# Main attention of a two-layer kernel: rows of maxima of two heads in one tile, a third score bank, and the maxima's banks shared

## What is computed

```python
q = (rmsnorm(h @ q_a_w.T) @ q_b_w.T)          # 16 heads: 128 plain + 64 rotary
kv_a = h @ kv_a_w.T                            # 64 latent + 16 x 64 rotary keys
q_pe, k_pe = apply_rope(q_pe), apply_rope(k_pe)
probs = softmax(qf @ kf.T * 192 ** -0.5)       # 1024 x 1024 for each head
main_out = (probs @ v) @ o_w.T
```

## Time and profile before

| | |
|---|---|
| median of 3 runs | 1565.17 us (1564.35 to 1569.16) |
| the profiled execution | 1566.81 us, its span 1565.0 us |
| PE busy | 1426.5 us (91%) in 7287 instructions |
| PEld / DVE / ACT / POOL busy | 54% / 59% / 48% / 35% |
| chain that ended last | PE 36%, DVE 6%, issue 3%, ACT 2% of the span |
| main attention | from about 310 to 930 us |

### The profile page before, as it was taken

The page is one execution under the profiler, slowest core; times in us unless marked ns, Lnnn a source line. Parts: engine busy times, 40 slices in busy tenths (PEclk is TensorE's granted clock), DMA queues, the critical chain, the costliest instruction groups (busy, mean ns, idle before and its releaser), DMA issues. The chain is left out here.

```text
span 1565.0 us, 20565 instructions
## 1 busy us (share of the span) xinstructions
PE 1426.5 (91%) x7287; PEld 841.9 (54%) x7350; DVE 926.7 (59%) x1719; ACT 747.3 (48%) x1368; POOL 548.9 (35%) x454
## 2 busy tenths in 40 slices
PE   6889999899999999999999968899579999879998
PEld 3533333355455555454545546788434444468887
DVE  5588776456666666666666344444458787544445
ACT  3457776654545454545453324233235555435553
POOL 4260162155565655656566522233200000101210
PEclk9979999999999999999999968899789999959999
DMA  7980000000000000000001011110076000101110
GB/s 292 179 114 1 2 21 7 1 1 0 1 1 0 1 1 1 1 1 1 1 1 42 0 41 39 36 55 27 1 168 93 1 1 1 50 21 41 41 41 27
DMA packets 20442, 53.04 MB, mean 34 GB/s; under 512 B 4630, under 2 KB 7464, under 8 KB 19123
## 3 DMA queue, kind: packets, MB, share of 16 engines
q1 hardware_dynamic: 20341, 51.73, 13.6%
HBM read 42.28 MB, written 8.39 MB: 32 GB/s over the span
## 5 line engine op out<-in xcount | busy, mean ns | idle before, releaser
L1631 POOL TENSOR_TENSOR Ps<-Ps,Pb 128x512 f32<-128x512 f32 x192 | 245.3, 1291 | 161.4 <-ACT Pb L1614 161.4
L1614 ACT ACTIVATE Pb<-bank 128x512 f32<-128x512 f32 x256 | 152.9, 597 | 287.5 <-PE bank L1603 235.0
L1575 DVE TENSOR_REDUCE mp<-bank 128x1 f32<-128x512 f32 x256 | 171.7, 687 | 141.6 <-PE bank L1568 139.7
L1062 DVE TENSOR_REDUCE mp<-bank 128x2 f32<-128x1024 f32 x128 | 153.6, 1222 | 48.4 <-PE bank L1054 48.0
L1121 ACT ACTIVATE Pb<-bank 128x512 f32<-128x512 f32 x256 | 133.2, 600 | 39.7 <-PE bank L1104 39.3
L1568 PE MATMUL bank<-qk1h,qk0h 128*128 128x512 f32 x256 | 135.7, 541 | 7.7 <-DVE mp L1575 7.7
L1600 PE MATMUL bank<-qk0h,qk1h 128*128 128x512 f32 x256 | 124.3, 486 | 6.1 <-DVE mrow L996 6.1
L1645 PE MATMUL bank<-Pb,kvx 128*64 128x512 f32 x512 | 124.0, 605 | 1.0 <-ACT Pb L1614 0.7
L1246 ACT ACTIVATE Pb<-bank 128x512 f32<-128x512 f32 x192 | 84.7, 489 | 80.2 <-PE bank L1233 57.4
L1214 DVE TENSOR_REDUCE mp<-bank 128x1 f32<-128x512 f32 (+1 forms) x192 | 97.8, 552 | 17.6 <-PE bank L1204 11.5
L1602 PE MATMUL bank<-qk0h,qk1l 128*128 128x512 f32 x256 | 101.2, 396 | 0.0
(11 more groups left out here) (341 smaller groups left out, 3265.5 us busy)
## 6 DMA issues: line engine op xcount, KB each, us to landing
wr<-wf SPq DMA_DIRECT2D x25, 256.0 KB, 2.6
wraw<-wf SPq DMA_DIRECT2D x8, 768.0 KB, 4.1
scratch<-stgr SPq DMA_DIRECT2D x4, 1024.0 KB, 3.9
scratch<-stg SPq DMA_DIRECT2D x4, 768.0 KB, 7.0
owT<-owT SPq DMA_DIRECT2D x1, 2048.0 KB, 9.9
qbn<-qbn SPq DMA_DIRECT2D x1, 1536.0 KB, 14.9
qstr<-scratch SPq DMA_DIRECT2D x12, 128.0 KB
kstr<-scratch SPq DMA_DIRECT2D x12, 128.0 KB
```

What stands on the lines that cost most here:

```text
L1062: e.tensor_reduce(mp[:, w % 3, :, j, kh], wide[slot][:], AX, ALU.max).then_inc(ring_ok, 1)
L1575: e.tensor_reduce(mp[:, u % 3, hd, j, kh:kh + 1], bank[b][:, 0:c], AX, ALU.max).then_inc(mp_ok[2], 1)
L1614: e.activation(Pbm[n % NPBM][:], bank[b][:], ACT.Exp, scale=SC0).then_inc(exp_ok[2], 1)
L1631: e.tensor_tensor(Ps[z][:], first, Pbm[n % NPBM][:], ALU.add).then_inc(sum_ok, 1)
```

## The change

1. Order (main_order, attention_order). The maxima of the next unit end one step earlier; "neg", "tr" and "row" come two steps earlier. Preparation parts get fixed steps: products at steps 1, 5, 9, 13, 17 and 21 of a pair's 32 (two rope parts of the keys first, then a latent part), "swap" at the same step, "turn" one later, a new step "sum" two later, "high" two, "low" four later. "project" is placed right behind a "pv", and its addition is a step "add" of its own, one score tile later. All of ctx and cadd lie in unit 0.
2. Rows. Both heads' rows are in one tile mrow, at rows 0 to 10 and 64 to 74; onesr has two blocks alike. The two score tiles of a key block get their fourth product together, behind the second head's third: two products of 64 rows each into two banks.
3. Banks. The score tiles use banks 2, 3 and 6. The turned maxima and half of the output products use banks 0 and 1, in one ring with the maxima (RINGM). ctx and cadd use bank 5.
4. Preparation in place. "turn" writes bank 7, "sum" is VectorE's, into bank 7, "high" and "low" read bank 7. So the next product waits for rp_lo.
5. The reciprocal goes to PSUM and is multiplied from there. The turns behind the attention use banks 2 and 3, and the first experts begin with the other pair of banks.

```diff
-PREP_TIMES = (0, 1, 2, None, 3, 4, 5, None, 6, 7, 8, None, 9, 10, 11, None, 12, 13, 14, None, 15, 16, 17, None, 18, 19)
+PRODUCT_AT = ((R0, 1), (R1, 5), (Q0, 9), (R2, 13), (Q1, 17), (R3, 21))
+FOLLOW = {"rope": (("product", 0, 1), ("swap", 0, 1), ("turn", 1, 0), ("sum", 2, 0), ("high", 2, 1), ("low", 4, 0)),
+          "lat": (("product", 0, 1), ("high", 0, 1), ("low", 1, 0))}
...
-        begin, last_max = (0, nk) if ahead == 2 else (3 * (u % 2), nk - 5)
+        begin, last_max = (0, nk) if ahead == 2 else (2 * (u % 2), nk - 6)
...
-        return [(0, [("den", u)]), (1, [("recip", u)]), (4, [("project", u, 0)]), (6, [("project", u, 1)])]
-    order = attention_order(16, 2, False, 2, 1, (2, 3, -4, -2), at_begin, at_step, evac, lead=False)
+        return [(1, [("den", u)]), (4, [("recip", u)]), (5, [("project", u, 0)]), (6, [("add", u, 0)]),
+                (9, [("project", u, 1)]), (10, [("add", u, 1)])]
+    order = attention_order(16, 2, False, 2, 1, (2, 3, -6, -4), at_begin, at_step, evac, lead=False, at_front=at_front)
...
-    BANK7 = {R0: (rp_cos, 4, -4), Q0: (rp_cos, 4, 1), R1: (lt_lo, 2, 1), R2: (rp_cos, 4, 2), Q1: (rp_cos, 4, 3),
+    BANK7 = {R0: (rp_lo, 4, 0), R1: (rp_lo, 4, 1), Q0: (rp_lo, 4, 2), R2: (lt_lo, 2, 1), Q1: (rp_lo, 4, 3),
              R3: (lt_lo, 2, 2)}
...
-                    e.activation(QKh[n][z][64:128, cs], Rt[64:128, :], ACT.Copy)
+                    e.activation(QKh[n][z][64:128, cs], bank[7][64:128, :], ACT.Copy)
...
-                    e.wait_ge(rp_sum, k)
-                    e.tensor_tensor(t12[:, 0, :], bank[7][:], cosT[:, cs], ALU.mult).then_inc(rp_cos, 1)
+                    e.tensor_tensor(bank[7][:], bank[7][:], cosT[:, cs], ALU.mult).then_inc(rp_cos, 1)
+                if what == "sum":
+                    e.wait_ge(rp_cos, k + 1)
+                    e.wait_ge(rp_sin, k + 1)
+                    e.tensor_tensor(bank[7][:], bank[7][:], t12[:, 1, :], ALU.add).then_inc(rp_sum, 1)
...
-                e.wait_ge(rp_lo, k)
-                e.tensor_tensor(Rt[:], t12[:, 0, :], t12[:, 1, :], ALU.add).then_inc(rp_sum, 1)
...
-    TILEM = tile_table(MAIN, lambda u: (2, 3))
+    TILEM = tile_table(MAIN, lambda u: (2, 3, 6))
...
+    RINGM, MAXNO, ringm_free = {}, {}, [ring_free[0], ring_free[0]]
+    for s_ in [("max", 0, *s) for s in max_steps(2, 0, False)] + MAIN:
+        if s_[0] in ("max", "tr", "project"):
+            b_ = len(RINGM) % 2
+            RINGM[s_] = (b_, ringm_free[b_])
...
-            e.wait_ge(b6_ok[2], B6M["row", u] + 1)
...
-        e.matmul(o, onesr[:], mrow[u % 2 * 2 + hd][:], start=False, stop=True).then_inc(st_mm[2], 1)
+        if hd:
+
+            if kt == 0:
+                e.wait_ge(b6_ok[2], B6M["row", u] + 1)
+                if u == 0:
+                    e.wait_ge(rows_ok, 5)
+            for h in range(2):
+                r = slice(64 * h, 64 * h + 64)
+                e.matmul(bank[TILEM["st", u, h, kt][1]][:], onesr[r, :], mrow[u % 2][r, :],
+                         start=False, stop=True).then_inc(st_mm[2], 1)
...
-        e.reciprocal(r, bank[4 + u % 2][:, 0:8]).then_inc(rec_ok, 1)
+        o = bank[4 + u % 2][:, 8:16]
+        e.reciprocal(o, bank[4 + u % 2][:, 0:8]).then_inc(rec_ok, 1)
...
+        b0, free = RINGM[s]
         e.wait_ge(rec_ok, 2 * u + 2)
+        e.wait_ge(*free)
```

More of the change, by code:

```diff
@@ L50, in max_steps, with attention_order @@
     return out
-def attention_order(nu, nh, causal, group, ahead, lag, at_begin, at_step, evac, lead=True):
+def attention_order(nu, nh, causal, group, ahead, lag, at_begin, at_step, evac, lead=True, at_front=lambda u, k: []):
     order, due, n = [], [], 0
@@ L60, in run_due @@
     def run_due():
-        for d in [d for d in due if d[0] <= n]:
+        for d in sorted((d for d in due if d[0] <= n), key=lambda d: d[1][0][0] != "pv"):
             due.remove(d)
@@ L86, in attention_order @@
                 order += unit_head(u + 1)[0]
+            order += at_front(u, k)
             due_now = 0
@@ L215, in causal_order @@
     return attention_order(32, 1, True, 4, 2, (2, 2, 0, 2), lambda u: [], at_step, lambda u: [(0, [("evac", u)])])
[L219 to L227, removed]
 FIRST = (R0, R1, R2, Q0, Q1, R3)
@@ L560, in turn_bank @@
     def turn_bank(n, half, k):
-        return bank[5 + k if (n, half) == (1, 1) else 2 * half + k]
+        return bank[(2, 5)[half] + k if n == 1 else 2 * half + k]
     def pe_turn(e, n, half):
+        if (n, half) == (1, 0):
+            e.wait_ge(exp_ok[2], 256)
         for j in range(4):
@@ L1354, in pe_prep @@
                 continue
-            if part != R0:
-                s, per, k = BANK7[part]
-                e.wait_ge(s, per * p + k)
-            elif p == 1:
+            s, per, k = BANK7[part]
+            e.wait_ge(s, per * p + k)
+            if part == R0 and p == 1:
                 e.wait_ge(exp_ok[0], 256)
-            else:
-                e.wait_ge(rp_cos, 4 * p)
             pe_part(e, p, part, bank[7][:], (0, 1))
@@ L1558, in pe_maxm @@
         _, u, hd, j, kh, c = s
-        b, before = MAXM[s]
+        b, free = RINGM[s]
         p = u // 2
@@ L1564, in pe_maxm @@
             e.wait_ge(key_hi, 2 * min(p, 1) + 2)
-        e.wait_ge(*((mp_ok[2], before + 1) if before is not None else ring_free[0]))
+        e.wait_ge(*free)
         qh, _, kh_, _ = tiles_of(2 * p + hd)
@@ L1594, in pe_stm @@
             e.wait_ge(key_lo, 2 * min(p, 1) + 2)
-            if u == 0:
-                e.wait_ge(rows_ok, 6)
-        e.wait_ge(*((exp_ok[2], before + 1) if before is not None else ring_free[1]))
+        if before is not None:
+            e.wait_ge(exp_ok[2], before + 1)
+        else:
+            e.wait_ge(*((ot_ok[0], 8) if b == 6 else ring_free[1]))
         qh, ql, kh, kl = tiles_of(2 * p + hd)
@@ L1691, in pe_project_out @@
             j = 2 * q + k
[L1692 removed]
+            for hd, b in ((0, b0), (1, 4 + u % 2)):
                 r = slice(64 * hd, 64 * hd + 64)
@@ L1746, in pe_cadd @@
         for k in range(2):
-            last = e.matmul(bank[6][:, 256:512], cT0[:, i % 4, k, :], wsp[:, 3, k, :], start=(k == 0), stop=(k == 1))
+            last = e.matmul(bank[5][:, 256:512], cT0[:, i % 4, k, :], wsp[:, 3, k, :], start=(k == 0), stop=(k == 1))
         last.then_inc(op_mm, 1)
```

105 lines of the change are left out of this document (61 added, 44 removed).

## The result

The changed kernel takes **1592.82 us** (median of 4 runs, 1589.09 to 1596.1) against 1565.98 of the kernel before beside it: a ratio of 1.0168, 95% interval 1.014 to 1.0196. The forecast was 1573. Slower was right, the size was not: the profiled execution (1596.1 us, span 1594.3, the longest of the four) is 29.3 us longer than that of before, where the sum said 7.6.

What follows compares the result with a forecast made beforehand. TensorE's own queue was taken as the bound. Row products +4.6, six regular pairs +7, first pair -3 and last pair -1 gave +7.6 us on the span of 1565.0: 1572.6, said as 1573, range 1547 to 1587.

Steps and rivals of the forecast that it cites:

- The cost of the row products: Main attention: 128 half-row pairs with their changes of tile shape cost 64.0 us against 59.4 for full rows, +4.6 us.
- the waits for bank 7: Main attention: the next projection waits until the low half has read bank 7; stalls of 0.8, 1.3 and 1.9 us per pair.
- the pattern's products fill gaps in the first pair: First pair of units: the pattern's output transpositions and products, spread between steps, fill the stall gaps, -3 us.
- the whole stall of 3.4 us per pair goes: Regular pairs: third score bank and earlier maxima remove all of TensorE's old stall, about 3.4 us per pair.
- maxima wait 0.6: Odd unit, two maxima per step: a ring of two banks gives small stalls, about 0.6 us a pair.
- idle time costs only itself: Main attention: new stalls entered the sum at their own length, 4.6 us per pair, with no term for the clock.
- the rivals with 0.198 and without overlap: Half-row pairs: entering costs as with fp32r weights, +11.9, 1585 us (chance 0.12); the halves don't overlap, +28, 1601 us (0.05).
- The products of a pair, 73.0: TensorE's products and returns to full tiles in one pair of the kernel before: together 73.0 of 76.4 us.
- three chains: Preparation from one projection to the next: first to second key rope, second to latent product, third rope to second latent product.
- The rival that the preparation is hidden: Main attention: low halves finish before TensorE's next projection; only 0.9 of 4.6 us per pair stay, 1551 us, chance 0.32.
- the third chain's wait: Third rope to second latent product: 6.8 us of TensorE's work, low half ends at 8.7, stall 1.9 us.
- The last pair, -0.4 with the rows: Last pair of units: prepares nothing and loses its row wait, but ends with two exponentials in a row, -1 us before rows.

Runs made afterwards that it cites:

- new order (9): Changed kernel with preparation in place undone, full-row fourth products, two score banks, maxima alone in banks 0 and 1, turns and output products in bank 6: 1545.56 us.
- kernel 7: Changed kernel with preparation in place undone and full-row fourth products; third score bank and shared ring kept: 1554.06 us, 0.9934 of the kernel before.
- kernel 1: Changed kernel with only the preparation in place undone (sum by GpSimd into Rt, bank 7 free after the cosine product): 1562.71 us, 0.9988 of the kernel before.
- kernel 8: As kernel 7, but bank 6 goes from the scores to the ring of maxima, turns and output products: 1535.38 us, 0.9815 of the kernel before.
- kernel 6: Kernel before with only half-row pairs in place of full-row fourth products; order, two score banks and preparation as there: 1617.79 us, 1.0336 of it.
- kernel 5: Changed kernel with the second latent and fourth rope products one value group later (steps 21 and 25 for 17 and 21): 1571.24 us, 1.0048 of the kernel before.
- kernel 13: Changed kernel with the second keys' copies at step 12 and low halves at step 29, not the begin: 1587.22 us, 1.0141 of the kernel before.
- kernel 15: Kernel 8 with the second keys' copies at step 12 and low halves at step 29: 1533.57 us, 0.9801 of the kernel before.

## Why the prediction was wrong in size

The kernel takes 20 us more than forecast. The cost of the row products and the waits for bank 7 came as placed. Three steps failed: that the pattern's products fill gaps in the first pair (-3; +9.1 measured), that the whole stall of 3.4 us per pair goes and maxima wait 0.6 (2.4 measured), and that idle time costs only itself (two stretches at half clock, 1.3 us each, and more in the first pair).

Kernels 9, 7 and 1 and the changed one make a ladder. Its first two steps take several things together: "new order" stands also for the multiply of the factors in PSUM and for the pattern's output in bank 5, and the step from 9 to 7 both gives the scores a third bank and puts turns and output products into the maxima's ring.

| kernel | us | first pair | its granted clock | from its third tile on | regular pair |
|---|---|---|---|---|---|
| before | 1565 | 81.8 | 0.98 | | 76.4 |
| new order (9) | 1545.6 | 81.7 | 0.99 | 73.5 | 73.8 |
| + third score bank, ring shared (7) | 1554.1 | 84.8 | 0.95 | 74.6 | 74.6 |
| + half-row pairs (1) | 1562.7 | 87.6 | 0.98 | 77.3 | 75.0 |
| + preparation in place (changed) | 1592.8 | 90.9 | 0.94 | 79.2 | 79.2 and 80.5 |

The fifth column is the rest of the first pair from the start of its third score tile. None of these kernels has half clock there, so it compares them without the clock. The kernel before has other work ahead of that tile.

- **Row products, +4.6: right.** The pair ends 0.32 behind its forerunner, the next product 0.43 behind the pair. A regular pair of kernel 1 less its 2.1 us of waits is 72.9 us, against 72.3 of kernel 8, which has full rows and no waits: 0.6, where 4.6/8 = 0.58 was forecast. The entering price of 0.105 us from the causal stage's bf16 rows was the right choice, and the rivals with 0.198 and without overlap fall. What the term left out is that two tiles end together. With two score banks that shows as 24.8 us of waits for exponentials (kernel 6); with three it is in the 8.6 us from kernel 7 to 1, next to 1.2 us more per pair at maxima and 1.6 less at output products.
- **The old stall of 3.4 us per pair goes: wrong, a third of it went.** By the distances of ends in a pair of the kernel before, 1.2 us of it stand at the row and 1.7 at two maxima (the rest in small pieces). TensorE's idle time over its six regular pairs, 392 to 850 us:

```profile
PE bank L1568 <- DVE mp L1575: 7.1, 12, 0.6
PE bank L1600 <- DVE mrow L996: 4.0, 12, 0.5
```

The earlier row removes the second line, and no score tile of the changed kernel waits for a row. The maxima's part stays: by the same distances it is 2.4 us per pair, in more and smaller pieces, little of it idle time. The earlier trace rows already had 24.9 us there against 11.6 for the row. It takes a third bank in the ring (kernel 8) to remove it.
- **The products of a pair, 73.0: 0.8 too high.** I had the output products right behind the value groups pay a change of shape, "still one change in and one out". They don't: the earlier trace rows show 64-column value groups and 64-row output groups each paying on the return to full tiles, and with the two side by side one return falls away, 4 x 0.2 = 0.8 per pair. 73.0 - 0.8 = 72.2; kernel 8 has 72.3.
- **Bank 7, 4.0 us per pair in three chains: right, chain by chain.** Forecast 0.8 (0.3 of it at a maximum), 1.3 and 1.9; found 0.52, 1.35 and 1.93 by the distances of ends. The rival that the preparation is hidden falls with it: no such wait is left in kernel 1, and there it is worth 30 us. One reading was too simple: the 1560 ns of L1496 are no price of two SBUF operands, since the same line took 864 ns on average for the queries, and L1498 684, in the kernel before.
- **The clock: not in the sum.** Two of the six regular pairs lost 1.3 us each to a stretch at half clock behind the third chain's wait. The rows of before had no idle time of 1.9 us in a regular pair from which to read it, but a forecast of an idle time of that size should have carried a bound for it.
- **The ring of two banks, 0.6 us per pair: too low by 1.8.** The regular pair has 2.4 us at maxima and 2.1 still in kernel 1. I worked with the mean of a step, 2.75 us of reductions against 2.9 of products; but pairs of maxima come back to back, and each further thing on VectorE ahead of a reduction shows. It is the ring: with full rows and two banks 0.85 are left, shared or not (kernels 7 and 9), with three nothing (kernel 8).
- Together a regular pair is 79.2 where 78.2 was said: -0.7 by the products, +1.7 by waits, and 1.3 more in two pairs. Against the sum that is 8.7 us over six pairs.
- **The first pair, -3: wrong, +9.1, and the largest error, 11.5 us** with its share of the row products. I argued that the pattern's products fill gaps. But they bring VectorE eight additions and the keys' work, and ScalarE eight copies, on the two engines that the in-place chains and the shared ring had just been made to depend on. From the third tile on, the ladder's shares are 1.1 for the third score bank with the shared ring, 2.7 for half-row pairs and 1.9 for the preparation in place. Ahead of that tile the new order takes 8.2, 10.2, 10.3 and 11.7 us in the four kernels, and 1.4 of the last is the clock (kernel 5 beside it). The wait there is the third maximum's, 2.0 us, for a reduction queued on VectorE behind the row and the keys' 2.5 us; kernel 13, which moves the keys' work, takes 6.3 us, and kernel 15 shows that with three ring banks the same item costs 1.4. That the pattern's additions and copies are what lengthens the rest is argued: no kernel here leaves them out.
- **The last pair, -0.4 with the rows: -1.2 found.** Fine. The pattern stage's 2.7 us ahead are no effect of the change that any run here shows.

Each of those shares depends on the steps below it in the ladder: half-row pairs cost 8.6 us in kernel 1, 19 in the changed one and 53 in the kernel before, with its order and two banks.

## What to carry to other kernels

A chain that computes in a PSUM bank in place holds the bank for as long as the chain's slowest queue; before giving up an SBUF copy for it, add up everything queued ahead of each link, and price the idle time at the end also by the clock. A freed bank should go where a wait stands: here the maxima's ring, not the scores, and 19 us lie between the two choices. Extra TensorE work did not fill gaps in the stage with the most work on the helper engines.

## What the runs showed of the hardware

- Half-row bf16 products between full fp32r ones: two in 0.32 us after the forerunner and 0.20 us more for the next full product, 0.52 in place of 2 x 0.232 = 0.46. The Trainium skill, page "TensorEngine Tiling (Array Packing)", Theoretical Speedup, has up to twice the speed for such products; this trace does not show it where they alternate with full tiles.
- A 64-column value group followed by a 64-row output group pays no return between them (the output group takes 1.06 us there, and 1.07 behind a full product).
- Idle stretches of 1.84 to 1.86 us at the same place, six in each of five kernels, were followed by 3.4 us at half clock in 10 of 30, and kernel 1 has such a stretch with no idle time ahead. What decides is open.
- The same work at the begin of the first pair took 11.7 us at a granted clock of 0.56 and 10.3 at 0.83.
